# Attention turns of a decoder layer: the first tile's scores ahead of the first projection, its exponentials ahead of the last probability copies, a weight block's high copy later

## The reference, cut to what matters

```
x = x + state_space(layernorm(x))                        # recurrence over the 4 steps of the first axis
x = x + cross_attention(layernorm(x), ctx)               # the change is here
x = x + butterfly_mlp(layernorm(x))                      # 512 -> 2048 -> 512

def cross_attention(query, context):                     # 16 heads of 32, 77 keys for each batch
    Q = (query @ Wq.T).reshape(B, T_q, 16, 32)
    K, V = (context @ Wk.T), (context @ Wv.T)
    scores = einsum('bqhd,bkhd->bhqk', Q, K) / sqrt(32)
    out = einsum('bhqk,bkhd->bqhd', softmax(scores), V).reshape(B, T_q, 512)
    return out @ Wo.T
```

## Time and profile before

| | |
|---|---|
| median of 3 runs | 2285.23 us (2284.19 to 2288.47) |
| the profiled execution, span | 2285.0 us |
| TensorE busy | 2217.8 us (97%), DVE 1696.3 (74%), ACT 1227.2 (54%), POOL 467.4 (20%) |
| attention turns g = 3 to 14 | 12 turns from 397.63 to 929.53 us, 44.28 to 44.36 us each |
| turn g = 2 | 352.10 to 397.63 us, of which 1.2 us more before O2 than in the others |
| turn g = 15, the last with scores | from 929.53 us |
| MLP stage | from about 1001 us to the end |

### The profile page before, as it was taken

The page is one execution under the profiler, slowest core; times in us unless marked ns, Lnnn a source line. Parts: engine busy times, 40 slices in busy tenths (PEclk is TensorE's granted clock), DMA queues, the critical chain, the costliest instruction groups (busy, mean ns, idle before and its releaser), DMA issues.

```text
span 2285.0 us, 41150 instructions
## 1 busy us (share of the span) xinstructions
PE 2217.8 (97%) x15910; PEld 1933.0 (85%) x15910; DVE 1696.3 (74%) x2854; ACT 1227.2 (54%) x2735; POOL 467.4 (20%) x578
## 2 busy tenths in 40 slices
PE   6998889999999999999999999999999999999999
PEld 4887677778878877778988989989989989889899
DVE  5666588888888888866857947858758669579567
ACT  2655566666676666554635535536446346355343
POOL 3531132222232222300030020200300300300203
PEclk8999999999999999999999999999999999999999
DMA  9888733332342332357676686785786676776765
GB/s 316 295 310 317 228 98 102 105 121 79 121 127 80 106 114 85 130 190 227 210 240 212 212 264 180 218 266 174 223 267 204 200 260 208 231 221 212 227 188 193
DMA packets 202090, 443.34 MB, mean 194 GB/s; under 512 B 32442, under 2 KB 70586, under 8 KB 200362
## 3 DMA queue, kind: packets, MB, share of 16 engines
q1 hardware_dynamic: 201898, 440.72, 60.0%
HBM read 341.66 MB, written 99.01 MB: 193 GB/s over the span
## 4 chain that ended last, share of the span: by engine, by line
PE 81%; ACT 8%; DMA 5%; DVE 4%; issue 1%; SPq 1%; POOL 0%; DVEq 0%; ACTq 0%; POOLq 0%
PE ps L441 69%; PE ps L1938 4%; DMA x_scratch<-xa 3%; PE ps L1906 2%; ACT es L1060 2%; ACT xn L906 2%; PE ps L1917 2%; PE ps L1869 1%; ACT wc_h L1016 1%; ACT pth L1034 1%; PE ps L1835 1%; DVE st L1256 1%; DMA wd_scratch<-stage 1%; DVE ptl L1293 1%; PE ps L1795 1%
## 5 line engine op out<-in xcount | busy, mean ns | idle before, releaser
L441 PE MATMUL ps<-ring,gh 128*128 128x256 f32 x3584 | 652.8, 284 | 0.1
L441 PEld LDWEIGHTS ps<-ring,gh 128*128 128x128 f32 x3584 | 558.3, 192 | 2.1 <-DVE gl L1293 1.5
L441 PE MATMUL ps<-xth,ring 128*128 128x512 f32 x1792 | 553.0, 389 | 0.0
L441 PE MATMUL ps<-ring,gl 128*128 128x256 f32 x1792 | 506.8, 283 | 0.0
L441 PEld LDWEIGHTS ps<-xth,ring 128*128 128x128 f32 x1792 | 336.4, 188 | 69.6
L1161 ACT ACTIVATE gh<-G 128x512 fp32r<-128x512 f32 x384 | 239.2, 629 | 218.7 <-PE ps L441 218.2
L441 PE MATMUL ps<-xtl,ring 128*128 128x512 f32 x896 | 348.6, 389 | 0.0
L441 PEld LDWEIGHTS ps<-ring,gl 128*128 128x128 f32 x1792 | 343.5, 192 | 0.0
L1293 DVE TENSOR_TENSOR gl<-G,gh 128x512 fp32r<-128x512 f32 x384 | 276.9, 733 | 50.5 <-ACT gh L1161 49.5
L849 POOL TENSOR_TENSOR es<-es,rinv 128x308 f32<-128x308 f32 x256 | 180.5, 736 | 422.0 <-DVE rinv L1467 422.0
L1144 ACT ACTIVATE G<-G,up_b 128x512 f32<-128x512 f32 x192 | 139.0, 724 | 221.9 <-DVE G L1579 221.9
(11 more groups left out here) (232 smaller groups left out, 4405.5 us busy)
## 6 DMA issues: line engine op xcount, KB each, us to landing
ring<-wup_scratch SPq DMA_DIRECT2D x224, 512.0 KB, 3.8
ring<-wdn_scratch SPq DMA_DIRECT2D x224, 512.0 KB, 3.6
X<-x_scratch SPq DMA_DIRECT2D x32, 1024.0 KB, 8.8
xa<-in_x SPq DMA_DIRECT2D x16, 1024.0 KB, 6.3
x_scratch<-xa SPq DMA_DIRECT2D x16, 1024.0 KB, 8.8
x<-x_scratch SPq DMA_DIRECT2D x16, 1024.0 KB, 5.5
x_scratch<-x SPq DMA_DIRECT2D x16, 1024.0 KB, 4.3
out_x<-X SPq DMA_DIRECT2D x15, 1024.0 KB, 7.8
```

Source lines behind the costliest of these rows:

```text
L441: mm = pe.matmul(bank, a, b, start=first and i == 0, stop=last and i == n - 1, skip_group_check=go_on)
```

## The change

On TensorE `scores(0)` stands ahead of `project(2, -2)` (S0 before O2). On DVE `shift(0)` stands right behind `lo_p(2, -1)`, ahead of the layer norm's moments and of `residual(2, -2)`. On ACT all of `exp(0)` stands ahead of all three copies `hi_p(3, -1)`; before, two copies were ahead of it and the third was inside it. And `high_weights(g)`, from turn 2 on, stands behind `hi_p(0, 0)` and `hi_x(2)`; before, it stood ahead of `hi_p(0, 0)` (in turn 15 it was already behind it).

```
-                        if t == 0:
-                            hi_p(3, -1, range(2, 3))
...
-                hi_p(3, -1, range(2 if has(0) else 3))
                 exp(0)
+                hi_p(3, -1)
...
-                if 2 <= g < NG - 1:
-                    high_weights(g)
...
                 hi_p(0, 0)
-                if g == NG - 1:
+                hi_x(2)
+                if 2 <= g < NG:
                     high_weights(g)
-                hi_x(2)
                 exp(2)
...
                 lo_p(2, -1)
+                shift(0)
                 if has(1) and g > 1:
                     moments2(g + 1)
                 residual(2, -2)
...
-                shift(0)
...
                 turn_p(2, -1)
+                scores(0)
                 project(2, -2)
...
-                scores(0)
                 turn_p(3, -1)
                 project(3, -2)
```

## The result

The changed kernel takes 2276.45 us (median of 5 runs, 2275.06 to 2278.93) against 2287.37 us for the kernel before in the same series (5 runs, 2284.19 to 2290.66). The ratio is 0.9947, 95% interval 0.9933 to 0.996: 10.9 us less by the medians. The profiled executions have 2273.2 and 2285.0 us, 11.8 less. A later series has 2277.84 us (6 runs) against 2287.18 (11 runs): 9.3 less.

The account below looks back on a forecast made before the run. TensorE was taken as the bound, with small waits of 1.35 us per 44.31 us attention turn. Gains of 9.3 (thirteen turns) and 3.4 (turn 15), less 0.4 (turn 1), made 12.3 us: 2273 us, range 2267 to 2279.

Parts of the forecast that it names:

- P2 to S0 unchanged at 1.58: TensorE, turn's start: tile 0's scores still wait for the queries' last low part, 1.58 us after the weight transposes start.
- A new wait of O3 for the residual, 0.15: TensorE: the next projection waits 0.15 us for DVE's residual, now later behind the shift and moments.
- S1 and the norm free: TensorE: tile 1's scores lose their 0.15 us wait for exponentials, the X transposes their 0.4 us wait for the layer norm.
- the walk: Step-by-step prediction of start times through turn 7 on TensorE, DVE and ACT, giving 0.72 us less per turn.
- P0 and O0: TensorE, mid-turn: ACT copies the weight transposes earlier, so the projection after them loses its 0.5 us wait for their low part.
- The weights' copy delays tile 2's exponentials and makes P1 wait 0.26: ACT: the moved copy pushes tile 2's exponentials from 599.2 to 600.67; later transposes' third bank waits 0.26 us.
- The sum of a turn, -0.72: Attention turn: net 0.72 us less, bounds 0.3 to 1.2; thirteen turns give 9.3 us.
- Turn 1, +0.4: Turn without projections: ACT's new order delays the third low part, a loss of 0.4 us, bounds 0 and 1.
- Turn 15, -3.4: Last attention turn: wait for values shrinks from 2.49 to 1.1 us and the clock stays up, gaining 3.4 us.
- Rival 3, falls set off by new waits: TensorE's clock falls in each of thirteen turns, making a turn 1.0 us longer: 2298 us; chance 0.04.
- The median: Whole kernel: runs' median forecast at 2273 us, taken as 0.2 us above the profiled execution.
- The total of the two profiles, -12.3: Whole kernel: profiled span falls by 12.3 us, from 2285.0 to 2272.7 us.

Follow-up runs that it names:

- the swap alone: Kernel before with only scores of tile 0 ahead of the projection on TensorE and shift of tile 0 ahead of the moments on DVE: 2284.9 us in the profile.
- the second series' profile: The changed kernel run again, unaltered, in a later series: 2277.84 us, ratio 0.9955 to the kernel before; 2277.4 us in the profile.
- the last kernel: Changed kernel plus four edits: residual ahead of moments, weights' copy behind X3's copy, old ACT order in turn 1, turn 15's statistics behind V0's low part: 2270.67 us, 0.9924.

## Why the prediction was right, point by point

- *P2 to S0 unchanged at 1.58:* 1.57. Right.
- *A new wait of O3 for the residual, 0.15:* the residual starts at 577.20, as walked, but P3 to O3 without a wait is 1.23, not the 1.28 of the earlier trace rows, so the wait is 0.23 (1.46 less 1.23). Shown by taking it away.
- *S1 and the norm free:* right. X0 stands 1.94 behind V0, and the norm is not in the list of waits. S1 is free with either edit alone (O3 to S1 2.94 and 2.92). The norm is covered without a loss only with both, which the walk contained (it moved both) and did not say: with the swap alone the norm is still late, with ACT's order alone V0 is.
- *P0 and O0:* V0 came 11.79 behind P2 (586.68 - 574.93 = 11.75 in the walk), X2 to O0 is 0.42 instead of 0.87 (walked: 0.36). Right to 0.06.
- *The weights' copy delays tile 2's exponentials and makes P1 wait 0.26:* the mechanism is right, its price 0.36. P1 came 29.47 behind P2 against 29.42 in the walk, the sums of tile 2 28.99 against 28.94, and the third bank began 0.26 late (601.26 against 600.06 + 0.94), just as walked. From there to S3 it took 0.56, against 0.47 where nothing waits (1.41 less 0.94): the term left out is 0.09 us that this third bank takes longer behind its wait.
- *The sum of a turn, -0.72:* -0.61 in turn 7, -0.64 as the mean of turns 3 to 14. (The walk's own numbers give 0.75: P1 at 604.35 and 14.14 more are 618.49, against 619.24.) P3 to O3 is 0.03 longer than walked (0.08 more wait on a step that needs 0.05 less), P1 to S3 0.09. They are the mis-sized terms, with X2 to O0; turns 2 to 14 gave 8.3 of the forecast 9.3.
- *Turn 1, +0.4:* +0.38, by luck. P3's third low part starts 1.35 later than before (11.55 behind the turn's start against 10.20; forecast 1.2) and V0 0.94 later (forecast 0.8): so far the mechanism is right. X0 is 1.5 later, not 0.4, since the clock falls behind V0's wait; that the kernel before had one fall more elsewhere in this turn hides it.
- *Turn 15, -3.4:* -2.46. The statistics started 10.03 us behind the turn's start, not 9.67, since P3's three low parts ended that much later than walked. V2 waits 1.46, not 1.1:

```profile
937.04 0.50 PE L1934 MATMUL ps<-pth,vh 128*128 128x512 f32 x1 [1.46 <-DVE aol L1289]
```

  The clock did stay up, 1.00 in the window that answers to the earlier trace rows:

```profile
937.00:943.00 6.00, 5.96 (x56) 1.00 0.14 53
```

  It stayed up here in all five profiles in which V2 waits 1.4 to 1.5 us, and fell in the kernel before and in those with the swap or the weights' copy alone (2.5 us). With ACT's order alone it stayed up behind 2.9 us, so that the short wait is what kept it up is not shown. From the turn's start to P0 2.95 us are gained; 0.5 of them are lost again behind it, where both kernels have a second fall (granted clock 0.50 over 6.8 us); in the changed kernel it begins 34.2 us behind the turn's start and not 36.1, and takes in more of the products there. In the second series' profile that fall is half as long, and the stretch takes 68.20.
- *Rival 3, falls set off by new waits:* in turns 2 to 14 of the changed kernel it did not happen, and the new waits there are 0.23 and 0.36. In turn 1 it did, behind V0's new wait of 1.58, which the prediction didn't count among them. ACT's order alone has it too: 1 us of wait in each turn, a fall in three of thirteen. My reason against it, that the waits of a turn were 1.35 in all and no turn fell, missed that they were split in four.
- *The median:* 2276.45 against 2273 forecast. The kernel before had 2287.37 in the same series, 2.1 above the median that the forecast started from; of the difference of 12.3 that it named, 10.9 came. The forecast also added 0.2 us to go from a profile to the median of the runs. But the time of a run is 1.9 us above the span of the same execution, in every run that has both (2275.06 and 2273.2 for the profiled one), so the 0.2 was no measure of this.
- *The total of the two profiles, -12.3:* -11.8, and this nearness is in part luck. 1.5 us of it lie ahead of turn 1, where nothing was changed; without them it is 10.3.

The busy time as a measure: the warning of the Trainium skill ("Trainium Kernel Development and Optimization", Performance Expectations) is borne out. By PE's busy time at most 0.57 us of a turn were to be had, 7.4 in thirteen; the changed kernel took 8.3 us out of turns 2 to 14, and the last kernel 1.25 (44.31 to 43.06) out of a turn.

## What to carry to other kernels

Edits to one software pipeline are not to be judged one by one: here one was worth 0.15 us a turn, one cost 0.45 and had falls of the clock behind its wait, and together they brought 0.5. Walk the whole turn with all of them, engine by engine, and look at each step for what is now its last release; for the turns 2 to 14 the walk gave every new wait at its place, to 0.1 us. An operation moved out of one wait needs a place where its engine is idle and the work behind it isn't yet wanted: ahead of tile 2's exponentials the weights' copy cost 0.36, behind X3's copy, where ACT was idle, nothing.

Measure a periodic kernel by its period, since a total of one run carries some 6 us from a stage that wasn't touched.

## What the runs showed that was not expected

The clock's fall does not follow from the length of one wait. With ACT's order alone, waits of 0.97 us at V0 were followed by a fall in three turns of thirteen, and a wait of 2.92 us at V2 in turn 15 by none:

```profile
965.24 0.50 PE L1936 MATMUL ps<-pth,vh 128*128 128x512 f32 x1 [2.92 <-DVE aol L1291]
```

In turn 2 the wait of 1.2 us behind P2 was followed by a fall in three kernels (O2, some 4.3 us behind P2, took 4.44 instead of 2.87) and by none in the others. What decides it was not tried. One such fall, with TensorE busy all through it, costs 1.6 to 1.7 us.

The start of the attention's turn 1 differed by 6.4 us between profiles of code that is the same up to there, with differing falls of the clock ahead of it.
